# A 32-tile attention pipeline: the last tile's powers, W, corrected v and state sums left out, and H of the tile ahead of it

## The chip, the cores and the metric

The kernel runs on the 8 cores of one Trainium2 chip. Each core takes 2 of 16 sequences (4096 rows of 1024), and no core talks to another. The metric is the device time of the slowest core, in microseconds. On each core TensorE (PE) does the matmuls and transposes, VectorE (DVE), ScalarE (ACT) and GpSimd (POOL) the elementwise work and the copies out of PSUM, and SyncE's queue (SP) and POOL issue the DMAs.

## What is computed

One pre-norm layer in two halves. The attention half works in chunks of 64 rows. A softmax inside the chunk is added to a tenth of what a running state M gives, and M is updated from row to row:

```python
Mk = einsum('bhde,bhe->bhd', M, k_t)
M = M - alpha * Mk[..., :, None] * k_t[..., None, :] + beta * v_t[..., :, None] * k_t[..., None, :]
...
attn_out = einsum('bhij,bhjd->bhid', attn, vi)
mem_out = einsum('bhid,bhde->bhie', qi, M)       # M of the chunks before
chunk_out = attn_out + 0.1 * mem_out
x = x + out @ Wo.T
```

The second half is a choice of rows by a controller, 64 small two-layer experts and a scatter back. It begins when the attention half is over.

## The kernel before

`phase_a` is the attention half and `phase_b` the expert half. A tile of phase A is one chunk of both sequences of the core (128 rows), and there are NT = 32 tiles, numbered from 0. The 64 row updates of a chunk are done at once: with the strictly triangular matrix A of alpha k k', the kernel forms the powers A[1] to A[4] and B[1] to B[4] (their transposes), adds the identity (AI), and multiplies six factors onto k. This gives W, and after the last factor Wf. With H, the sum over earlier tiles, `k_by_h` gives a correction of v, and RHS is the corrected v. `state_h` and `state_m` multiply Wf and RHS into the tile's contribution to H and to M.

All engines run one software pipeline, written out by hand: the loop over i from -1 to 34 works on tile i (projections k, v, q), tile j = i-1 (`gram_and_scores`), tile u = i-2 (powers, factors 0 to 3, `row_sums`, `queries`, `values`) and tile e = i-3 (factors 4 and 5, states, and the output projection `wo_part`). So step 32 has no projections (u=30, e=29, j=31), step 33 has u=31 and e=30, and step 34 has only e=31. Each engine goes through its own list in order, and semaphores order the engines against each other.

Names that are used below:

- `power_a`, `power_b`: 32 matmuls of 64x64 into psX on PE, copied by ACT (L411, L415). `factor`: 32 matmuls into psW on PE (L630), copied to W or Wf by DVE (L829). `state_h` L642 and `state_m` L653 write psY; DVE adds them to H_sb (L868) and M_sb (L880). POOL scales M_sb into Ms_sb (L381), which `queries` reads.
- `row_sums` (L677) waits, among others, for RHS in `s_rhs`. psY is one PSUM tile, shared by `k_by_h`, `state_h`, `state_m`, `row_sums`, `queries` and `values`. ACT takes its logarithm (L475), then the exponential (L477); POOL makes Pn from them (L391); `queries` (L700) and `values` (L684) fill psY again; `o_copy` (L435, ACT) moves it to o_fm, and `wo_part` (L569, 16 matmuls of 512 columns a tile, in two halves) multiplies by Wo. DVE adds x to each half (`x1_half`, L836), and SP stores it to x1d.
- From step 33 on, rows of phase B are prepared in phase A: `choice_stats` (L118, L119, L121, DVE) and `choice_ln` (L129, L131, ACT) for tiles 0 and 1 in step 33 and 2 and 3 in step 34, `choice_norm` (L137, DVE) in step 34. In ACT's list both `choice_ln` of step 33 stand ahead of `o_copy(31)`, and the second waits for `choice_stats(1)`, which stands behind `x1_half(30, 1)` in DVE's list.
- `cast` (L354): POOL's DMAs that write the experts' weights in bf16.
- SP ends its list with a wait until the last x1 stores have landed (L324, L325). Behind it the engines meet (L938), and PE's first work of phase B is `y_turn` (L1152).

Of the kernel before, what the change touches and what calls it, by code (L numbers as in the profile page):

```python
# [140 lines left out]
def phase_a(nc, ctx, sb, ps, sem, env):  # L141
# [73 lines left out]
    with ExitStack() as pa:  # L215
# [111 lines left out]
        def pool(g):  # L327
# [28 lines left out]
            for i in range(0, NT + 3):  # L356
# [36 lines left out]
                if 0 <= j < NT:  # L393
                    g.wait_ge(s_g, j + 1)
                    g.tensor_tensor(heads(A[0][:, :]), heads(g_sb[:, :]), by_mask(mlo), ALU.mult).then_inc(s_mask, 1)
                cast(u, 6)
                if 0 <= j < NT:
                    g.tensor_tensor(heads(B[0][:, :]), heads(g_sb[:, :]), by_mask(mup), ALU.mult).then_inc(s_mask, 1)
# [3 lines left out]
        def act(s):  # L402
# [35 lines left out]
            for i in range(-1, NT + 3):  # L438
                u, e, j = i - 2, i - 3, i - 1
                proj = 0 <= i < NT  # L440
                solve = 0 <= u < NT
# [29 lines left out]
                if solve:  # L471
                    s.wait_ge(s_pden, u + 1)
                    if u > 0:
                        s.wait_ge(s_pn, u)
                    s.activation(rden[:], psY, AF.Ln).then_inc(s_lden, 1)  # L475
                    s.wait_ge(s_lden, u + 1)
                    s.activation(rden[:], rden[:], AF.Exp, scale=-1.0).then_inc(s_rec, 1)  # L477
# [3 lines left out]
                if 0 <= j < NT:  # L481
                    s.wait_ge(s_pg, j + 1)
                    s.copy(heads(g_sb[:, :]), gram_scores[:, :, 0, :]).then_inc(s_g, 1)
                    s.activation(heads(PT[j % 2][:, :]), gram_scores[:, :, 1, :], AF.Exp, scale=0.125).then_inc(s_exp, 1)  # L484
# [9 lines left out]
        def pe(t):  # L494
# [108 lines left out]
            def power_a(u, k):  # L603
# [6 lines left out]
                if k == 4 and u + 1 < NT:  # L610
                    t.wait_ge(s_g, u + 2)
                    t.wait_ge(s_exp, u + 2)
# [34 lines left out]
            def state_m(e):  # L647
                t.wait_ge(s_h, e + 1)
# [24 lines left out]
            def row_sums(u):  # L673
                t.wait_ge(s_ptm, u + 1)
                t.wait_ge(s_rhs, u + 1)
# [38 lines left out]
            for i in range(-1, NT + 3):  # L714
                u, e = i - 2, i - 3
                proj = 0 <= i < NT
                solve = 0 <= u < NT
                ends = 0 <= e < NT

# [6 lines left out]
                if ends:  # L726
                    factor(e, 4)
# [5 lines left out]
                if ends:  # L733
                    factor(e, 5)
# [7 lines left out]
                if ends:  # L742
                    state_h(e)
# [5 lines left out]
                if ends:  # L749
# [14 lines left out]
                if solve:  # L764
                    power_b(u, 3)
                    factor(u, 0)
                    row_sums(u)
# [23 lines left out]
                if solve:  # L791
                    power_b(u, 4)
                    queries(u)
# [3 lines left out]
                if solve:  # L797
                    power_a(u, 5)
                    factor(u, 3)
                    values(u)  # L800

        def dve(v):
# [48 lines left out]
            for i in range(-1, NT + 3):  # L851
                u, e = i - 2, i - 3
                proj = 0 <= i < NT
                solve = 0 <= u < NT
                ends = 0 <= e < NT
                if ends:
# [9 lines left out]
                if ends:  # L866
# [9 lines left out]
                if ends:  # L876
# [545 lines left out]
```

## Time and profile before

| what | us |
|---|---|
| median of 3 runs | 1398.43 (1396.72 to 1401.19) |
| the profiled execution, its own time | 1394.15 |
| span of its slowest core (core 5) | 1392.3 |
| spans of the 8 cores | 1382.8 to 1392.3 |
| mean granted clock of core 5 | 0.943 |
| PE, DVE, ACT, POOL busy in the span | 83%, 70%, 58%, 48% |

A row of the timeline has its start in us from the span's start, its length, engine, line, operation, output<-inputs, shapes, the count that it merges, and in brackets the idle time of the engine ahead of it with what ended it. The granted clock is TensorE's: 0.50 is 1.2 GHz and 1.00 is 2.4 GHz. Ends of matmuls are modelled; "issue" is idle time in which the engine waited for nothing that the profile shows.

### The profile page before, as it was taken

The page shows a single profiled execution, that of the slowest core. Times are in us where ns is not written, and L with a number is a line of the kernel's source. Part 1 is how long each engine was busy: PE and PEld are TensorE (multiplying, and loading weights), DVE is VectorE, ACT ScalarE, POOL GpSimd, SP SyncE. Part 2 cuts the span into 40 slices and gives each one's busy share as a digit, 9 for nine tenths or more (in the row PEclk, how much of TensorE's full clock was granted, in tenths as well). Part 3 has the DMA queues.
Part 4 walks back from the last instruction along what each step waited for, and adds up shares of the span by engine and source line. Part 5 has one row for each costly group of instructions (what it writes and reads, how often), then busy time and mean ns, then how long its engine had stood idle before and what let it go on. Part 6 is the DMA issues. An engine that isn't in the chain of part 4 may idle for free. (4 is left out here: it accounts for less than half of the span.)

```text
span 1392.3 us, 68142 instructions; the slowest of 8 cores (1382.8 to 1392.3 us)
## 1 busy us (share of the span) xinstructions
PE 1148.8 (83%) x28864; PEld 692.5 (50%) x28864; DVE 980.6 (70%) x1389; ACT 810.8 (58%) x1187; POOL 672.1 (48%) x566
## 2 busy tenths in 40 slices
PE   1578988889899988889899888885677779887798
PEld 0245555555555555555555555553344556544665
DVE  3167777677777777777777777765778587785776
ACT  0155656555565555555565555654249776488775
POOL 4166766776767766777667766675101000011000
PEclk9799999999999999999999999996569799988999
DMA  9912222222222222222222222123134485750947
GB/s 160 149 44 45 43 51 51 52 48 49 47 51 55 45 49 53 47 53 43 52 50 53 50 47 40 30 34 79 23 94 143 134 263 164 217 184 35 312 135 235
DMA packets 75158, 122.09 MB, mean 88 GB/s; under 512 B 13408, under 2 KB 38000, under 8 KB 74864
## 3 DMA queue, kind: packets, MB, share of 16 engines
q1 hardware_dynamic: 48128, 92.30, 21.8%
q0 software_dynamic: 26736, 25.44, 13.6%
q8 instruction: 237, 3.88, 1.1%
q14 instruction: 57, 0.47, 0.1%
HBM read 117.93 MB, written 41.94 MB: 115 GB/s over the span
## 5 line engine op out<-in xcount | busy, mean ns | idle before, releaser
L829 DVE CAST W<-psW 128x1024 bf16<-128x1024 f32 x160 | 195.5, 1222 | 112.6 <-PE psW L630 112.4
L415 ACT CAST B<-psXY 128x1024 bf16<-128x1024 f32 x128 | 129.9, 1015 | 74.0 <-PE psXY L597 74.0
L1095 POOL TENSOR_TENSOR psel<-permT_sb,gmask_sb 128x256 bf16<-128x256 bf16 x32 | 20.1, 628 | 260.8 <-DVE permT_sb L1327 235.9
L411 ACT CAST A<-psXY 128x1024 bf16<-128x1024 f32 x128 | 129.8, 1014 | 21.2 <-PE psXY L597 21.0
L517 PE MATMUL psD<-wv_sb,xnf 128*128 128x512 bf16 x512 | 128.8, 386 | 13.6 <-DMA wv_sb<-wvT 13.6
L540 PE MATMUL psD<-wq_sb,xnf 128*128 128x512 bf16 x512 | 128.6, 385 | 11.8 <-DMA wq_sb<-wqT 6.4
L508 PE MATMUL psD<-wk_sb,xnf 128*128 128x512 bf16 x512 | 123.6, 386 | 14.6 <-DMA wk_sb<-wkT 11.8
L825 DVE TENSOR_TENSOR AI<-A,eye 128x1024 bf16<-128x1024 bf16 x160 | 131.1, 834 | 1.8 <-ACT A L411 1.3
L569 PE MATMUL psD<-wo_sb,o_fm 128*128 128x512 bf16 x512 | 131.3, 391 | 0.7 <-issue 0.6
L376 POOL TENSOR_TENSOR kt<-kraw,rk 128x1024 bf16<-128x1024 f32 x32 | 60.8, 1902 | 134.4 <-ACT rk L461 134.4
L1108 ACT CAST R<-P 128x1024 bf16<-128x1024 f32 (+1 forms) x128 | 110.1, 905 | 8.3 <-PE P L1187 6.2
L391 POOL TENSOR_TENSOR Pn<-PT,rden 128x1024 bf16<-128x1024 bf16 x32 | 68.6, 2142 | 91.1 <-ACT rden L477 91.1
L1340 DVE CAST R<-P 128x512 bf16<-128x512 f32 x128 | 81.2, 685 | 28.5 <-PE P L1214 28.2
L597 PEld LDWEIGHTS psXY<-A,B 64*64 64x64 bf16 x5120 | 57.1, 110 | 76.0 <-issue 72.9
L597 PE MATMUL psXY<-A,B 64*64 64x64 bf16 (+1 forms) x5120 | 74.9, 194 | 17.1 <-ACT PT L484 7.9
L630 PE MATMUL psW<-W,AI 64*64 64x64 bf16 x5120 | 75.7, 197 | 14.6 <-DVE W L829 7.7
L435 ACT CAST o_fm<-psXY 128x1024 bf16<-128x1024 f32 x32 | 32.4, 1012 | 94.3 <-PE psXY L684 94.3
L1144 ACT COPY ring<-P 128x1024 bf16<-128x1024 bf16 x64 | 64.6, 1012 | 37.0 <-PE P L1228 37.0
L429 ACT CAST q_tm<-psD 128x512 bf16<-128x512 f32 x64 | 37.6, 587 | 82.1 <-PE psD L540 82.1
L363 POOL TENSOR_TENSOR PT<-PT,mj 128x1024 bf16<-128x1024 bf16 x32 | 68.4, 2136 | 30.7 <-DVE AI L825 30.7
L372 POOL TENSOR_TENSOR sq_sb<-kraw 128x1024 f32<-128x1024 f32 x32 | 60.6, 1893 | 45.9 <-ACT kraw L419 28.4
L1187 PE MATMUL P<-psel,xy 64*128 64x256 bf16 x512 | 58.6, 310 | 28.5 <-ACT R L1108 22.9
(138 smaller groups left out, 2578.7 us busy)
## 6 DMA issues: line engine op xcount, KB each, us to landing
ring<-f1d SPq DMA_DIRECT2D x64, 256.0 KB, 4.0
ring<-f2d SPq DMA_DIRECT2D x64, 256.0 KB, 5.0
out<-ring SPq DMA_DIRECT2D x64, 256.0 KB, 3.4
xy<-x SPq DMA_DIRECT2D x68, 128.0 KB, 2.4
f1d<-f1w POOLq DMA_DIRECT2D x128, 64.0 KB, 2.6
f2d<-f2w POOLq DMA_DIRECT2D x128, 64.0 KB, 2.7
x1d<-x1b SPq DMA_DIRECT2D x64, 128.0 KB, 2.4
xy<-x1d SPq DMA_DIRECT2D x32, 256.0 KB, 3.5
```

The source lines that it names most:

```text
L411: s.copy(A[k][:], psX).then_inc(s_a, 1)
L415: s.copy(B[k][:], psX).then_inc(s_b, 1)
L508: ins = t.matmul((psD0, psD1)[hf][:, :], xn_fm[i % 2][:, kc * 128:(kc + 1) * 128], wk_sb[:, kc * 1024 + hf * 512:kc * 1024 + hf * 512 + 51 ...
L517: ins = t.matmul((psD0, psD1)[hf][:, :], xn_fm[i % 2][:, kc * 128:(kc + 1) * 128], wv_sb[:, kc * 1024 + hf * 512:kc * 1024 + hf * 512 + 51 ...
L540: ins = t.matmul((psD0, psD1)[hf][:, :], xn_fm[i % 2][:, kc * 128:(kc + 1) * 128], wq_sb[:, kc * 1024 + hf * 512:kc * 1024 + hf * 512 + 51 ...
L569: ins = t.matmul((psD0, psD1)[hf][:, :], o_fm[:, oc * 128:(oc + 1) * 128], wo_sb[:, oc * 1024 + hf * 512:oc * 1024 + hf * 512 + 512], star ...
L597: ins = t.matmul(psX[c:c + 64, hr * 64:hr * 64 + width], left[k][r:r + 64, hr * 64:hr * 64 + 64], right[k][r:r + 64, hr * 64:hr * 64 + width],
L630: ins = t.matmul(psW[c:c + 64, hr * 64:hr * 64 + 64], AI[k][r:r + 64, hr * 64:hr * 64 + 64], w_old, start=True, stop=True, tile_position=( ...
L825: v.tensor_tensor(heads(AI[k][:, :]), heads(A[k][:, :]), by_mask(eye2), ALU.add).then_inc(s_ai, 1)
L829: v.tensor_copy((Wf if k == 5 else W[k % 2])[:], psW[:, 0:1024]).then_inc(s_w, 1)
L1108: s.copy(gather_place(n, q)[:, 0:h, :, :], gathered_ps(q)[:, 0:h, :, :]).then_inc(s_ga, 1)
L1340: v.tensor_copy(place(2 * p)[:, 4 * hf:4 * hf + 4, :, :], half_tiles(P[u % 3][:, 0:512])).then_inc(s_iv, 1)
```

## The change

The flag `solve` no longer holds for tile 31 and `state` (factors 4 and 5, `state_m`) no longer holds for tile 31 either; `state_h` and the sum into H stop after tile 29. `row_sums`, `queries` and `values` go by a flag of their own, `attend`, that still holds for tile 31. Two waits take the place of ones that would never be met: `row_sums(31)` waits for the sum into M_sb of tile 30 (`s_m`), and `state_m(30)` waits itself for Wf, RHS and the o_copy of tile 30. The masks A[0], B[0] of tile 31 and the copy g_sb that feeds them go as well.

```diff
@@ pool: masks of tile 31
-                if 0 <= j < NT:
+                if 0 <= j < NT - 1:
                     g.wait_ge(s_g, j + 1)
                     g.tensor_tensor(heads(A[0][:, :]), heads(g_sb[:, :]), by_mask(mlo), ALU.mult).then_inc(s_mask, 1)
...
-                if 0 <= j < NT:
+                if 0 <= j < NT - 1:
                     g.tensor_tensor(heads(B[0][:, :]), heads(g_sb[:, :]), by_mask(mup), ALU.mult).then_inc(s_mask, 1)
@@ act
-                solve = 0 <= u < NT
+                solve = 0 <= u < NT - 1
+                attend = 0 <= u < NT
...
-                if solve:
+                if attend:
                     s.wait_ge(s_pden, u + 1)
...
-                    s.copy(heads(g_sb[:, :]), gram_scores[:, :, 0, :]).then_inc(s_g, 1)
+                    if j < NT - 1:
+                        s.copy(heads(g_sb[:, :]), gram_scores[:, :, 0, :]).then_inc(s_g, 1)
@@ pe: power_a, state_m, row_sums
-                if k == 4 and u + 1 < NT:
-                    t.wait_ge(s_g, u + 2)
+                if k == 4:
+                    if u + 2 < NT:
+                        t.wait_ge(s_g, u + 2)
                     t.wait_ge(s_exp, u + 2)
...
-                t.wait_ge(s_h, e + 1)
+                if e < NT - 2:
+                    t.wait_ge(s_h, e + 1)
+                else:
+                    t.wait_ge(s_w, 6 * e + 6)
+                    t.wait_ge(s_rhs, e + 1)
+                    t.wait_ge(s_o, e + 1)
...
-                t.wait_ge(s_rhs, u + 1)
+                if u < NT - 1:
+                    t.wait_ge(s_rhs, u + 1)
+                else:
+                    t.wait_ge(s_m, u)
@@ pe: the loop
-                solve = 0 <= u < NT
+                solve = 0 <= u < NT - 1
+                attend = 0 <= u < NT
                 ends = 0 <= e < NT
+                state = 0 <= e < NT - 1
...
-                if ends:
+                if state:
                     factor(e, 4)
...
-                if ends:
+                if state:
                     factor(e, 5)
...
-                if ends:
+                if 0 <= e < NT - 2:
                     state_h(e)
...
-                if ends:
+                if state:
                     state_m(e)
...
                     factor(u, 0)
+                if attend:
                     row_sums(u)
...
+                if attend:
                     queries(u)
...
                     factor(u, 3)
+                if attend:
                     values(u)
@@ dve: the loop
-                solve = 0 <= u < NT
+                solve = 0 <= u < NT - 1
                 ends = 0 <= e < NT
-                if ends:
+                state = 0 <= e < NT - 1
+                if state:
                     v.wait_ge(s_pa, 5 * e + 5)
...
-                if ends:
+                if 0 <= e < NT - 2:
                     v.wait_ge(s_ph, e + 1)
                     v.tensor_add(H_sb[:], H_sb[:], psY).then_inc(s_h, 1)
...
-                if ends:
+                if state:
                     v.wait_ge(s_pm, e + 1)
```

How the engines' lists stand now is seen best at their ends. Line numbers of the changed kernel are higher (L569 is L571, L630 L633, L653 L661, L677 L688, L684 L695, L700 L711, L829 L846, L836 L853, L880 L898, L1152 L1170). PE's list before, from `queries(31)` to the first work of phase B:

```order
L700 MATMUL psXY<-kaq,Ms_sb 64x64 x32
L569 MATMUL psD<-wo_sb,o_fm 128x512 x8
L597 MATMUL psXY<-A,B 64x32 x32
L630 MATMUL psW<-W,AI 64x64 x32
L684 MATMUL psXY<-Pn,vt 64x64 x32
L630 MATMUL psW<-W,AI 64x64 x64
L642 MATMUL psXY<-RHS,Wf 64x64 x32
L653 MATMUL psXY<-Wf,RHS 64x64 x32
L569 MATMUL psD<-wo_sb,o_fm 128x512 x16
L938 UNCONDITIONAL_BRANCH
```

And PE's list now, from the beginning of step 33 (factors 4 and 5 of tile 30):

```order
L633 MATMUL psW<-W,AI 64x64 x64
L661 MATMUL psXY<-Wf,RHS 64x64 x32
L688 MATMUL psXY<-PT,onesblk 128x512 x2
L571 MATMUL psD<-wo_sb,o_fm 128x512 x8
L711 MATMUL psXY<-kaq,Ms_sb 64x64 x32
L571 MATMUL psD<-wo_sb,o_fm 128x512 x8
L695 MATMUL psXY<-Pn,vt 64x64 x32
L571 MATMUL psD<-wo_sb,o_fm 128x512 x16
L956 UNCONDITIONAL_BRANCH
```

The 16 matmuls of `wo_part(31)` stood behind two factors and both state products, and stand now right behind `values(31)`; ten of the fourteen groups of matmuls that stood ahead of `wo_part(30)` in step 33 are gone. DVE's list before, from `x1_half(30, 1)` on:

```order
L836 TENSOR_TENSOR x1b<-x,psD 128x512
L825 TENSOR_TENSOR AI<-A,eye 128x1024
L118 BN_STATS bst_y<-xy 128x6
L119 BN_STATS bst_y<-xy 128x6
L121 BN_AGGR mv_y<-bst_y 128x2
L858 TENSOR_TENSOR AI<-psXY,eye 128x16x32
L829 CAST W<-psW 128x1024 x2
L829 CAST Wf<-psW 128x1024
L868 TENSOR_TENSOR H_sb<-H_sb,psXY 128x1024
L880 TENSOR_TENSOR M_sb<-M_sb,psXY 128x1024
L137 TENSOR_SCALAR xy<-xy,mv_y,rstd_y 128x1024 x2
```

DVE's list now, from the last sum into M_sb (tile 30) on:

```order
L898 TENSOR_TENSOR M_sb<-M_sb,psXY 128x1024
L853 TENSOR_TENSOR x1b<-x,psD 128x512
L118 BN_STATS bst_y<-xy 128x6
L119 BN_STATS bst_y<-xy 128x6
L121 BN_AGGR mv_y<-bst_y 128x2
L853 TENSOR_TENSOR x1b<-x,psD 128x512
L118 BN_STATS bst_y<-xy 128x6
L119 BN_STATS bst_y<-xy 128x6
L121 BN_AGGR mv_y<-bst_y 128x2
L137 TENSOR_SCALAR xy<-xy,mv_y,rstd_y 128x1024 x2
```

The six operations between the choice's second statistics and its first norms are gone, and so is the AI sum between `x1_half(30, 1)` and the statistics; the order of what is left is as it was.

## Rows read from the trace of the kernel before

**Rows 1.** Timeline of core 5, end of step 33 to phase B.

```profile
991.34 1.90 PE L569 MATMUL psD<-wo_sb,o_fm 128*128 128x512 bf16 x8
...
993.35 0.69 DVE L836 TENSOR_TENSOR x1b<-x,psD 128x512 bf16<-128x512 f32 x1 [0.64 <-PE psD L569]
...
994.55 0.69 DVE L118 BATCH_NORM_STATS2 bst_y<-xy 128x6 f32<-128x512 bf16 x1
...
996.74 0.99 ACT L435 CAST o_fm<-psXY 128x1024 bf16<-128x1024 f32 x1
...
1004.84 0.64 PE L653 MATMUL psXY<-Wf,RHS 64*64 64x64 bf16 x32 [1.49 <-DVE H_sb L868]
...
1005.41 6.14 PE L569 MATMUL psD<-wo_sb,o_fm 128*128 128x512 bf16 x16
...
1011.66 0.69 DVE L836 TENSOR_TENSOR x1b<-x,psD 128x512 bf16<-128x512 f32 x1 [0.20 <-PE psD L569]
...
1014.90 1.01 PE L1152 MATMUL P<-ident_bf,xy 128*128 128x128 bf16 x8 [3.35 <-PEq L938]
```

**Rows 2.** Timeline of core 5, first part of step 33.

```profile
974.47 0.64 PE L630 MATMUL psW<-W,AI 64*64 64x64 bf16 x32 [0.86 <-DVE W L829]
...
975.23 1.23 DVE L829 CAST Wf<-psW 128x1024 bf16<-128x1024 f32 x1 [1.01 <-PE psW L630]
...
978.94 0.64 PE L653 MATMUL psXY<-Wf,RHS 64*64 64x64 bf16 x32 [0.49 <-DVE H_sb L868]
...
979.77 1.22 DVE L880 TENSOR_TENSOR M_sb<-M_sb,psXY 128x1024 bf16<-128x1024 bf16 x1 [0.37 <-PE psXY L653]
...
981.14 1.90 POOL L381 TENSOR_TENSOR Ms_sb<-M_sb,b 128x1024 bf16<-128x1024 bf16 x1 [6.92 <-DVE M_sb L880]
...
983.26 0.59 PE L677 MATMUL psXY<-PT,onesblk 128*128 128x512 bf16 x1
...
984.82 0.59 PE L677 MATMUL psXY<-PT,onesblk 128*128 128x512 bf16 x1 [0.97 <-issue]
```

**Rows 3.** Timeline of core 5, step 32: the softmax chain and a quarter of Wo.

```profile
956.81 1.03 PE L677 MATMUL psXY<-PT,onesblk 128*128 128x512 bf16 x2
...
958.00 1.02 ACT L475 ACTIVATE rden<-psXY 128x1024 f32<-128x1024 f32 x1 [0.49 <-PE psXY L677]
...
959.11 1.06 ACT L477 ACTIVATE rden<-rden 128x1024 f32<-128x1024 f32 x1
...
960.38 2.13 POOL L391 TENSOR_TENSOR Pn<-PT,rden 128x1024 bf16<-128x1024 bf16 x1 [3.04 <-ACT rden L477]
...
960.61 1.87 PE L569 MATMUL psD<-wo_sb,o_fm 128*128 128x512 bf16 x4
...
961.24 1.03 ACT L484 ACTIVATE PT<-psXY 128x1024 bf16<-128x1024 f32 x1
...
962.42 0.56 PE L597 MATMUL psXY<-A,B 64*64 64x64 bf16 x32
```

**Rows 4.** Busy time by engine, granted clock (PEclk), DMA share, GB/s in stretches of 3 us.

```profile
987.00:990.00 3.00, 3.00 (x70) 1.37 (x68) 1.41 (x2) 1.74 (x2) 2.06 (x1) 0.50 0.00 0
...
996.00:999.00 3.00, 0.65 (x32) 0.54 (x32) 1.98 (x4) 1.40 (x3) 0.00 (x0) 0.65 0.00 0
```

**Rows 5.** POOL's last casts in the timeline of core 5.

```profile
990.02 1.52 POOL L354 DMA_DIRECT2D f2d<-f2w  x3
```

**Rows 6.** DMA issues on the page: count, KB each, median us from issue to landing.

```profile
f2d<-f2w POOLq DMA_DIRECT2D x128, 64.0 KB, 2.7
```

**Rows 7.** Chain that ended last, first selection stretch of phase B: start, us, what.

```profile
1030.18 1.02 ACT R L1108
...
1035.52 1.02 ACT R L1108
...
1050.26 1.01 ACT R L1108
...
1054.34 1.00 ACT R L1108
```

## The prediction

> **What bounds the kernel now.** I read the end of phase A first, since the change touches nothing ahead of step 32. The timeline of the end of step 33 and of step 34 gives the last link: the last `x1_half` starts at 1011.66, its store has to land, the engines meet, and PE starts phase B at 1014.90, which is 3.24 us behind that start [rows 1]. Nothing of phase B can begin earlier, so phase B moves one for one with the last `x1_half`. That in turn waits for PE's `wo_part(31)`, which runs from 1005.41 to 1011.55; and this stands in PE's list behind `state_m(31)` at 1004.84 [rows 1]. Its own input o_fm was ready at 997.73, when `o_copy(31)` ended (996.74 + 0.99) [rows 1]. So 7.7 us of the tail (1005.41 - 997.73) is time in which `wo_part(31)` waits for factors and states that no later tile reads. I then followed step 33 backwards in the same way.
>
> **The change, part by part.** All times are of core 5.
>
> *Step 32.* POOL loses two masks, ACT the copy g_sb (about 1 us, as its neighbour L484). Exp(31) then starts 0.9 us earlier. `power_a(30, 4)`, which waits for it, started at 962.42; Exp ended at 962.27 and the four matmuls of Wo ahead of it on PE ended at 962.48 [rows 3]. The two covers end together, so with the first gone PE is still held by the second: I take 0. If the Wo matmuls ran at the full clock they would take about 1.0 (half of the 1.90 for eight in [rows 1]) instead of 1.87, and up to 0.8 us would be won; that is the upper bound. POOL's next operation behind the masks waits for AI[4] of tile 30, which DVE makes at the end of the step; 0.
>
> *Step 33, up to the sum into M.* The chain of factors of tile 30 alternates between PE and DVE: factor 5 starts on PE at 974.47 when DVE's copy of W is done, and Wf is copied from 975.23 to 976.46 [rows 2]. The powers of tile 31 lay in the gaps of it, so this part does not move. After it, `state_m(30)` started at 978.94, having waited for the sum into H [rows 2]. Now it waits only for Wf. An engine takes up work some 0.15 us behind another's end (POOL at 981.14 behind the sum at 980.99) [rows 2]; I allow 0.25, so it starts at 976.7. That is 2.2 us won. The sum into M follows 0.83 later (978.94 to 979.77), so from 977.55 to 978.75.
>
> *From M to Wo of tile 30.* Before, `row_sums(31)` came at 983.26 behind `k_by_h`, a power, a factor and RHS [rows 2]. Now it needs the sum into M alone: 978.9, 4.3 us earlier. In step 32 the logarithm started 1.19 us behind `row_sums`, the exponential 1.11 behind that and Pn 1.27 behind that [rows 3], which puts Pn from 982.5 to 984.6. Ms is made from 978.9 to 980.8 (1.90 in [rows 2]). PE runs the first 8 matmuls of `wo_part(30)` from 979.75. At the half clock 4 of them took 1.87 [rows 3], which with the modelled end of the last taken off is 0.43 each, so 8 take 3.4; at the full clock 8 took 1.90 with that end, so 1.75 [rows 1]. Then `queries(31)` for 0.65, then the second 8. At the half clock `wo_part(30)` ends at 987.25; at the full clock at 983.7 (the queries wait until 981.3 for the logarithm).
>
> *A wait that takes over.* `values(31)` could end by 985.3 to 988, and `o_copy(31)` behind it. But ACT has the second `choice_ln` ahead of `o_copy(31)`. Before, `x1_half(30, 1)` started at 993.35, `choice_stats(1)` at 994.55 (0.60 of that is the AI sum that now goes) and `o_copy` 2.19 later [rows 1]. From now on that is 0.60 + 2.19 = 2.8 us from `x1_half(30, 1)` to `o_copy(31)`, and another 1.2 (0.99 and a wait) until `wo_part(31)` starts, in which PE has nothing. In the kernel before this was hidden under the factors of tile 31.
>
> - Half clock throughout: `x1_half(30, 1)` 987.4, `o_copy` 990.2, `wo_part(31)` 991.35, which is 14.1 us earlier than 1005.41. 16 matmuls at 0.427 are 6.8, the last `x1_half` at 998.4, phase B at 1001.6: 13.3 us won.
> - Full clock throughout: 983.8, 986.6, 987.8; 16 matmuls take 3.5, but DVE becomes the limit: `x1_half(31, 0)` at 989.7, `choice_stats(3)` (0.6 + 1.6 us), last `x1_half` at 991.9, phase B at 995.1: 19.8 won.
>
> Which of them holds is read from the granted clock. In 987 to 990 it was 0.50 (1.2 GHz) with PE busy all three microseconds, and the next eight Wo matmuls at 991.34 ran at the full clock [rows 1, 4]; in 996 to 999, where PE was busy for 0.65 us of 3, it fell to the half clock (mean 0.65) [rows 4]. The 16 matmuls of `wo_part(31)` took 6.14, 0.9 less than 7.0 at the half clock with the modelled end, so the clock rose near their end [rows 1]. Now PE is busy without a gap from 978.9, so I expect the clock to rise at about 983 to 986, somewhere in `wo_part(30)`, to fall in or just behind the gap of 3 to 4 us ahead of `wo_part(31)`, and to rise again in it. With the rise at 983.3: `wo_part(30)` ends at 985.75, `o_copy(31)` 988.65, `wo_part(31)` from 989.85 for 5.2 to 6.2, last `x1_half` between 995.3 and 996.0, phase B at 998.5 to 999.2, 15.7 to 16.4 won. With the rise just too late for the second half of `wo_part(30)`: 13.3 to 14.5. I take the middle of the two, 15.2 us.
>
> The Trainium skill, "TensorE: Matmul & The Clock Gate", section "The HAM clock gate", says that the throttled clock is the default and that activity releases it. By that rule a kernel with less PE work keeps the half clock longer, and the sum would be the 13.3 us of the first line; the trace agrees with it in that the clock fell behind an idle stretch [rows 4].
>
> **Sum.** 2.2 (to `state_m`) + 2.1 more (to `row_sums`, together 4.3) + 10.9 more from there to phase B (in which two factors, their copies, H and M of tile 31 were 7.7, powers and factors between the Wo matmuls the rest) = 15.2. Phase B is unchanged. The profiled execution (1394.15, span 1392.3) would come to 1379.0; it lies 4.3 below the median, so against the median I predict 1398.4 - 15.2 = 1383.2.
>
> **The rivals.**
>
> - *Full clock through the tail*: 19.8 us, 1378.6. For it: Wo ran at the full clock at 991.34 [rows 1]. Against: PE has less to do ahead of `row_sums` now, and an idle gap ahead of `wo_part(31)`. 0.12.
> - *Half clock, and stalls of the sequencer on top*: PE had idle times put down to "issue" in step 33, in the middle of groups of like matmuls (0.97 between the two of `row_sums`) [rows 2]. At 13.3 less one or two such stalls of 1 to 2 us each: 9 to 12 won, 1386 to 1389. Against: PE's list now has 194 matmuls from the start of step 33 to phase B, where it had 802. 0.15.
> - *Phase A's end is held by another*: POOL's list ends with a wait for its casts. They were issued by 991.54 and land 2.7 us behind issue [rows 5, 6], so by 994.2, and they stand behind Pn in POOL's list, which should now end at 984.6: with the same 1.5 and 2.7, 988.8. That is ahead of the stores in each case. Only if the casts didn't move and landed much later would the gain stop; as no change, 1398. 0.03.
> - *The other side, a slower kernel*: in phase B's selection stretch a turn takes 5.34 us at the half clock (1030.18 to 1035.52) and 4.08 at the full clock (1050.26 to 1054.34) [rows 7]. If, entered 15 us earlier and otherwise, the stretch stayed at the half clock, each turn would cost 1.26 us more. The gain is used up after 12 turns, and the kernel is slower by over 0.3% (4.2 us) from 16 turns on; the stretch has 16 tiles in each half of phase B, about 13 of them at the full clock now, so both halves would have to lose it: 26 turns, 33 us, 1416. Phase B's own work sets its clock, so 0.02.
> - *Partly*: a wait that I don't see gives half of it back: 1391. 0.05.
>
> **How the numbers follow.** My forecast has 0.63 (13.3 to 17, that is 1381.4 to 1385.1). The others are 0.12, 0.15, 0.03, 0.02 and 0.05. A run of this kernel lies within 2 to 3 us of its median (1396.72 to 1401.19), and the slowest of eight cores counts, each with its own clock. The range that leaves out no more than 2 in 10 reaches from the full-clock case (1378.6) to one with a stall (1388): 1378.0 to 1388.3. 0.3% (4.2 us) is about what a measurement of this kernel can tell from no change. Faster by more: 0.63 + 0.12 + 0.15 + 0.05 = 0.95; I say 0.94. Within: 0.04. Slower: 0.02.
>
> **What would show the steps right or wrong.** On core 5 relative to the copy of Wf of tile 30 (then 975.23): `state_m(30)` 1.5 us behind it; `row_sums` 3.7; Pn 7.3; `o_copy(31)` between 11.4 and 15.0, ended in its wait by mv_y of DVE and not by PE; `wo_part(31)` 1.2 behind that, with a mixed clock; last `x1_half` to phase B 3.2. From Wf to phase B 24.5 us instead of 39.7. Wrong would be: `o_copy(31)` released by `values`; "issue" gaps inside the groups of step 33; a selection stretch of phase B with more turns at 0.50; or a time from the last `x1_half` to phase B above 3.5 us.

## The result and the profile after

The changed kernel took 1384.2 us (median, the fastest 1382.15), the kernel before 1397.58 in the four runs beside it. Runs in which the cores of a die ran at a lower clock (one of four of the changed kernel here, 1431.15 us) are left out of every median and ratio of this document. The ratio is 0.9897, with a 95% interval of 0.9868 to 0.9925; in a later measurement (e11) it was 0.9886 [0.9869, 0.9903]. By the means of the runs that is 14.4 us less (1383.57 for 1397.98) and 16.0 us less (1382.78 for 1398.80); the forecast was 15.2 less, 1383.2 us, in a range of 1378.0 to 1388.3.

The profiled execution took 1382.15 us itself. The page's first lines, of its slowest core (core 0): the span, and for each engine its busy time, share and instructions (PE had 28864 matmuls before, 608 more).

```profile
span 1380.5 us, 66842 instructions; the slowest of 8 cores (1365.7 to 1380.5 us)
PE 1145.0 (83%) x28256; PEld 687.5 (50%) x28256; DVE 966.6 (70%) x1373; ACT 801.9 (58%) x1178; POOL 668.3 (48%) x564
```

The timeline of core 5 (span 1373.5 us here), the core that [rows 1, 2] show, from step 33 to phase B: the columns are start, duration, engine, line, operation, and in brackets the idle time before with what ended it. Here L571 is `wo_part`, L661 `state_m`, L688 `row_sums`, L711 `queries`, L695 `values`, L435 `o_copy`, L853 `x1_half`, L1170 the start of phase B.

```profile
970.65 1.23 DVE L846 CAST Wf<-psW 128x1024 bf16<-128x1024 f32 x1 [1.01 <-PE psW L633]
972.24 0.64 PE L661 MATMUL psXY<-Wf,RHS 64*64 64x64 bf16 x32 [1.71 <-DVE Wf L846]
973.07 1.22 DVE L898 TENSOR_TENSOR M_sb<-M_sb,psXY 128x1024 bf16<-128x1024 bf16 x1 [1.19 <-PE psXY L661]
974.43 1.01 PE L688 MATMUL psXY<-PT,onesblk 128*128 128x512 bf16 x2 [1.55 <-DVE M_sb L898]
975.24 3.14 PE L571 MATMUL psD<-wo_sb,o_fm 128*128 128x512 bf16 x8
977.97 2.13 POOL L391 TENSOR_TENSOR Pn<-PT,rden 128x1024 bf16<-128x1024 bf16 x1 [0.66 <-ACT rden L478]
978.94 1.90 PE L571 MATMUL psD<-wo_sb,o_fm 128*128 128x512 bf16 x8
980.06 1.52 POOL L354 DMA_DIRECT2D f2d<-f2w  x3
980.77 0.44 PE L695 MATMUL psXY<-Pn,vt 64*64 64x64 bf16 x32
980.95 0.69 DVE L853 TENSOR_TENSOR x1b<-x,psD 128x512 bf16<-128x512 f32 x1 [0.26 <-PE psD L571]
983.23 0.29 ACT L129 ACTIVATE rstd_y<-mv_y,cst 128x1 f32<-128x1 f32 x1 [1.87 <-DVE mv_y L121]
983.73 1.00 ACT L435 CAST o_fm<-psXY 128x1024 bf16<-128x1024 f32 x1
985.09 5.04 PE L571 MATMUL psD<-wo_sb,o_fm 128*128 128x512 bf16 x16 [3.87 <-ACT o_fm L435]
990.62 0.66 DVE L853 TENSOR_TENSOR x1b<-x,psD 128x512 bf16<-128x512 f32 x1
995.38 1.01 PE L1170 MATMUL P<-ident_bf,xy 128*128 128x128 bf16 x8 [5.25 <-PEq L956]
```

`state_m` now waits for the copy of Wf, and `row_sums` for the sum into M. The row to read twice is that of ACT at 983.23. `values` ended at 981.21, but ACT took `o_copy` up at 983.73 only, behind the second `choice_ln`, which had waited 1.87 us for mv_y of DVE. So PE stood for 3.87 us ahead of `wo_part(31)`. And from the last `x1_half` (990.62) to phase B it took 4.76 us, not the 3.24 of [rows 1].

The windows of the same core: PE (with its instructions), PE's weight loads, DVE, ACT and POOL, then the granted clock, the share of time in which the DMA engines were busy, and GB/s moved.

```profile
972.00:975.00 3.00, 1.21 (x34) 0.81 (x35) 1.22 (x1) 0.00 (x0) 0.57 (x1) 0.50 0.00 0
975.00:978.00 3.00, 3.00 (x9) 0.98 (x7) 0.00 (x0) 2.08 (x2) 2.34 (x4) 0.54 0.14 17
978.00:981.00 3.00, 3.00 (x70) 1.51 (x72) 2.15 (x5) 0.22 (x1) 3.00 (x3) 1.00 0.31 70
984.00:987.00 3.00, 1.91 (x5) 0.72 (x6) 1.88 (x4) 1.22 (x3) 0.00 (x0) 0.60 0.01 2
987.00:990.00 3.00, 3.00 (x12) 1.08 (x10) 1.49 (x3) 0.00 (x0) 0.00 (x0) 0.83 0.00 0
```

The clock rose near the end of the first half of `wo_part(30)`, fell by the start of `wo_part(31)` (mean 0.60 in 984 to 987; PE had just stood for 3.87 us), and rose in it.

In what follows all times are counted from the start of DVE's copy of Wf of tile 30 and are medians over the eight cores of one execution: so what the cores differ by in the 970 us ahead of it (up to 12 us within one execution) drops out. How finely the table can be read is seen where a kernel stands in it twice: changed and e11 differ by 0.1 us at phase B, 0.4 at the last `x1_half` and 0.7 at `o_copy`, e8 and e12 by 0.2, 0.5 and less than 0.1.

| kernel | `row_sums` | Pn | `o_copy` | `wo_part(31)` | last `x1_half` | phase B | last two apart |
|---|---|---|---|---|---|---|---|
| before | 8.08 | 12.57 | 21.31 | 29.97 | 35.96 | 39.18 | 3.21 |
| changed | 3.78 | 7.32 | 13.75 | 15.10 | 20.65 | 24.22 | 3.57 |
| e1, o_copy first | 3.78 | 7.32 | 11.45 | 12.85 | 18.18 | 23.89 | 5.78 |
| e2, masks kept | 3.79 | 7.32 | 13.74 | 15.16 | 20.64 | 24.35 | 3.71 |
| e3, step 34 only | 8.05 | 12.57 | 20.97 | 22.37 | 28.00 | 31.36 | 3.23 |
| e4, H of tile 30 kept | 5.91 | 9.45 | 15.45 | 16.81 | 22.47 | 26.20 | 3.73 |
| e5, casts early | 3.79 | 7.32 | 13.39 | 14.78 | 20.25 | 23.20 | 2.93 |
| e6, e1 and e5 | 3.79 | 7.32 | 10.90 | 12.28 | 17.63 | 20.69 | 3.10 |
| e7, PE filled | 3.60 | 6.72 | 9.66 | 11.03 | 15.59 | 19.83 | 4.24 |
| e8, softmax ahead | -2.38 | 1.09 | 7.28 | 8.81 | 13.73 | 16.94 | 3.23 |
| e9, POOL longer | 3.78 | 7.32 | 11.43 | 12.84 | 18.15 | 22.52 | 4.37 |
| e10, Ms on DVE | -2.35 | 1.18 | 7.71 | 9.18 | 14.64 | 17.57 | 2.93 |
| e11, changed again | 3.78 | 7.32 | 13.05 | 14.60 | 20.28 | 24.12 | 4.07 |
| e12, as e8, timed | -2.41 | 1.18 | 7.27 | 8.83 | 14.23 | 17.14 | 2.93 |

(The last column is the median of the cores' own differences.) From before to changed the stretch is 15.0 us shorter (39.18 - 24.22). What lies behind it stayed: from phase B's first matmul to the end of the core it is 377.5 us before, 377.8 in the changed kernel and 376.8 in e11 (medians of the cores, which differ among themselves by 5 to 8 us).

### The profile page after: what moved, and what is told of

The parts are those of the page before. It is cut to its first block and busy times, and to the rows that moved or that the text cites. A ratio compares the mean times of both kernels' runs of the same rounds, so it can differ in the third digit from the quotient of the medians.

```text
span 1380.5 us, 66842 instructions; the slowest of 8 cores (1365.7 to 1380.5 us)
## 1 busy us (share of the span) xinstructions
PE 1145.0 (83%) x28256; PEld 687.5 (50%) x28256; DVE 966.6 (70%) x1373; ACT 801.9 (58%) x1178; POOL 668.3 (48%) x564
## 5 line engine op out<-in xcount | busy, mean ns | idle before, releaser
L846 DVE CAST W<-psW 128x1024 bf16<-128x1024 f32 x155 | 189.3, 1221 | 111.2 <-PE psW L633 110.9
L415 ACT CAST B<-psXY 128x1024 bf16<-128x1024 f32 x124 | 125.8, 1015 | 69.9 <-PE psXY L599 69.9
L519 PE MATMUL psD<-wv_sb,xnf 128*128 128x512 bf16 x512 | 129.0, 386 | 13.6 <-DMA wv_sb<-wvT 13.6
L411 ACT CAST A<-psXY 128x1024 bf16<-128x1024 f32 x124 | 125.8, 1014 | 20.6 <-PE psXY L599 20.1
L571 PE MATMUL psD<-wo_sb,o_fm 128*128 128x512 bf16 x512 | 130.7, 390 | 5.8 <-ACT o_fm L435 3.9
L435 ACT CAST o_fm<-psXY 128x1024 bf16<-128x1024 f32 x32 | 32.4, 1012 | 93.6 <-PE psXY L695 93.6
L633 PE MATMUL psW<-W,AI 64*64 64x64 bf16 x4960 | 73.5, 196 | 12.2 <-issue 6.1
```

Of the source, the lines that this page charges most:

```text
L411: s.copy(A[k][:], psX).then_inc(s_a, 1)
L415: s.copy(B[k][:], psX).then_inc(s_b, 1)
L519: ins = t.matmul((psD0, psD1)[hf][:, :], xn_fm[i % 2][:, kc * 128:(kc + 1) * 128], wv_sb[:, kc * 1024 + hf * 512:kc * 1024 + hf * 512 + 51 ...
L571: ins = t.matmul((psD0, psD1)[hf][:, :], o_fm[:, oc * 128:(oc + 1) * 128], wo_sb[:, oc * 1024 + hf * 512:oc * 1024 + hf * 512 + 512], star ...
L633: ins = t.matmul(psW[c:c + 64, hr * 64:hr * 64 + 64], AI[k][r:r + 64, hr * 64:hr * 64 + 64], w_old, start=True, stop=True, tile_position=( ...
L846: v.tensor_copy((Wf if k == 5 else W[k % 2])[:], psW[:, 0:1024]).then_inc(s_w, 1)
```

## The experiments

### Which part gave what: e1 to e4

Lines marked - are the changed kernel's, + the experiment's, unless said otherwise.

**e1** moves the second `choice_ln` of step 33 on ACT behind `o_copy(31)`.

```diff
                 if 0 <= e < NT:
                     o_copy(e)
+                    if i == NT + 2:
+                        choice_ln(s, env, 1)
...
                     choice_ln(s, env, 2 * (i - NT - 1))
-                    choice_ln(s, env, 2 * (i - NT - 1) + 1)
+                    if i > NT + 1:
+                        choice_ln(s, env, 2 * (i - NT - 1) + 1)
```

> The changed kernel with ACT's o_copy(31) moved ahead of the second choice_ln of step 33. My theory: in the changed kernel o_copy(31) is held by the statistics of choice tile 1 and not by values(31), so o_copy(31) comes about 2.5 us earlier against the copy of Wf of tile 30 (median of the cores 13.75 us behind its start now, then 11.3), wo_part(31) likewise, and phase B 2 to 3 us earlier (24.2 to about 21.8 behind that start). Rival, that values(31) or PE's own list holds it: nothing moves. Rival, that DVE takes over as the limit (its norms and third statistics ahead of x1_half(31, 0)): wo_part(31) is earlier, phase B by less than 1 us.

`o_copy`, `wo_part(31)` and the last `x1_half` came 2.2 to 2.5 us earlier (1.6 to 2.1 against e11), as they should; phase B came 0.3 earlier (23.89 for 24.22). The timeline and the waits of core 5, PE's and then SP's (what waited, for what, us in all, times, longest):

```profile
982.00 1.52 POOL L354 DMA_DIRECT2D f2d<-f2w  x3
984.32 1.01 ACT L435 CAST o_fm<-psXY 128x1024 bf16<-128x1024 f32 x1 [0.52 <-PE psXY L698]
985.78 3.61 PE L574 MATMUL psD<-wo_sb,o_fm 128*128 128x512 bf16 x16 [1.58 <-ACT o_fm L435]
991.04 0.66 DVE L856 TENSOR_TENSOR x1b<-x,psD 128x512 bf16<-128x512 f32 x1
```
```profile
PE P L1173 <- PEq L959: 7.0, 1, 7.0
SPq L959 <- PEq L959: 2.6, 1, 2.6
```

`o_copy` is now released by `values` (PE psXY), so the wait behind `choice_ln` was real. But SP, whose wait for the last store ended 2.6 us before the engines met, was not last any more. Both rows name PE's own queue, which had been done with its list for 7 us: a releaser by inference, and not the cause. Something else held the end of phase A, in all eight cores at the same place (23.8 to 24.4 us behind the start of the copy of Wf, with 5.34 to 7.12 from the last `x1_half` to phase B).

**e2** makes the two masks and g_sb of tile 31 again, which nothing reads.

```diff
-                if 0 <= j < NT - 1:
+                if 0 <= j < NT:
...
-                    if j < NT - 1:
+                    if j < NT:
                         s.copy(heads(g_sb[:, :]), gram_scores[:, :, 0, :]).then_inc(s_g, 1)
...
-                    if u + 2 < NT:
+                    if u + 1 < NT:
                         t.wait_ge(s_g, u + 2)
```

> The changed kernel with what it took from step 32 put back: the copy g_sb on ACT and the two masks of tile 31 on POOL. My theory: both were covered, so the time from row_sums of tile 30 to the first copy of W in step 33 stays the same within 0.3 us, and the time from the copy of Wf of tile 30 to phase B stays at 24.2 us. Rival, that Exp(31) held PE in step 32: 0.5 to 0.9 us more in step 32.

Behind Wf the two kernels are alike (24.35 and 24.22). Ahead of it, step 32 from the start of `row_sums(30)` to Wf took 18.12 us before, 18.24 in e2, 17.36 in the changed kernel and 17.30 in e11: leaving these operations out gave 0.8 us. The other runs agree: e3, which keeps them, shows 18.10, and the nine others without them 17.10 to 17.51. So the expectation of no more than 0.3 us was wrong. It did not come through Exp(31): `power_a(30, 4)` starts 5.61 us behind `row_sums(30)` before and in e2, and 5.54 and 5.52 in the other two. It lies in `queries(30)`, whose 32 matmuls took 1.55 us before, 1.73 in e2, 0.79 and 0.69 in the changed kernel and e11 (medians of the cores). The timelines of the kernel before (core 5, L700), of e2 (core 1) and of the changed one (core 5):

```profile
964.77 0.56 PE L700 MATMUL psXY<-kaq,Ms_sb 64*64 64x64 bf16 x24
966.45 0.31 PE L700 MATMUL psXY<-kaq,Ms_sb 64*64 64x64 bf16 x8 [1.12 <-issue]
```
```profile
960.67 0.56 PE L711 MATMUL psXY<-kaq,Ms_sb 64*64 64x64 bf16 x24
962.09 0.31 PE L711 MATMUL psXY<-kaq,Ms_sb 64*64 64x64 bf16 x8 [0.86 <-issue]
```
```profile
961.18 0.69 PE L711 MATMUL psXY<-kaq,Ms_sb 64*64 64x64 bf16 x32
```

The gap in the middle is an "issue" one: the profile shows nothing that PE waited for. Without the masks it is gone in most cores, not in all (core 1 of the changed kernel still has 0.54 us of it, and 1.42 for the group). POOL's casts then also go out together and earlier; whether that is why was not tried.

**e3** is the kernel before with only what belongs to tile 31 left out in step 34 (factors 4 and 5, their copies, H and M); its powers, masks and first factors are computed, and so is H of tile 30. Against the kernel before:

```diff
+                state = 0 <= e < NT - 1
...
-                if 0 <= e < NT:
+                if state:
                     factor(e, 4)
...
-                if 0 <= e < NT:
+                if state:
                     state_m(e)
```

> The kernel before with only the parts of step 34 left out (factors 4 and 5, both state products and both sums of tile 31); step 33 stays whole. My theory: wo_part(31) then starts when o_copy(31) is done, 21.3 + 1.3 = 22.6 us behind the start of the copy of Wf of tile 30 instead of 30.0, so about 7.4 us are won, and from there 5.2 to 6.2 us to the last x1_half: phase B at about 31.5 to 32 instead of 39.2. The rest of the 15 us, about 7.5, is then step 33's. Rival, that the tail's gain was given back by the clock (more of wo_part(31) at the half clock): phase B at 33 or more.

`row_sums` and Pn stay where they were (8.05, 12.57), `o_copy` within 0.4 (20.97). `wo_part(31)` comes 7.6 earlier, right behind `o_copy`, and phase B 7.8: just the 7.7 that the prediction read from [rows 1]. The other 7.2 of the 15.0 come from step 33.

**e4** computes H of tile 30 again, which only M of tile 31 would need.

```diff
             def state_m(e):
-                if e < NT - 2:
-                    t.wait_ge(s_h, e + 1)
-                else:
-                    t.wait_ge(s_w, 6 * e + 6)
-                    t.wait_ge(s_rhs, e + 1)
-                    t.wait_ge(s_o, e + 1)
+                t.wait_ge(s_h, e + 1)
...
-                if 0 <= e < NT - 2:
+                if state:
                     state_h(e)
...
-                if 0 <= e < NT - 2:
+                if state:
                     v.wait_ge(s_ph, e + 1)
```

> The changed kernel with H of tile 30 still computed (state_h(30) on PE, the sum into H on DVE, and state_m(30) behind it). My theory: both lie on the path to row_sums(31), so the sum into M starts 2.1 us later (4.54 instead of 2.42 us behind the start of the copy of Wf), and phase B comes 2.1 us later: 26.3 instead of 24.2. Rival, that later waits (Pn, choice statistics) swallow it: phase B later by less than 1 us.

M starts at 4.54 again (2.42 without H), Pn 2.13 later, phase B at 26.20: H of one tile was worth 2.0 us, nearly undiminished to the end. So of the 15.0 us 7.8 are step 34's (e3) and 2.0 are H's (e4). The other 5.2 (31.36 - 26.20) come from what else left step 33, the powers, factors 0 to 3, `k_by_h` and RHS of tile 31; no run takes these apart.

### What holds the end of phase A: e5 to e7, and e9

Two things were left for e1's lost 2.2 us: POOL, whose program ends with a wait for its last casts, and something on PE's side, which the profile names.

**e5** issues POOL's casts of step 33 (parts 3 to 7) right behind part 2, ahead of Ms and Pn; **e6** is e5 with e1's edit.

```diff
                 cast(u, 2)
+                if i == NT + 1:
+                    for part in range(3, 8):
+                        cast(u, part)
...
-                cast(u, 3)
-                cast(u, 4)
+                if i != NT + 1:
+                    cast(u, 3)
+                    cast(u, 4)
```

> The changed kernel with POOL's last five weight casts (tile 31, parts 3 to 7) issued in step 33 ahead of Ms and Pn instead of around and behind them. In the changed kernel and in e1 the last packets of POOL's casts moved 11.1 to 11.5 us ahead of phase B in every core looked at, while the time from the last x1_half to phase B went from 2.9 to 7.1 us. Theory A: POOL, with its wait for the casts, is the last to reach the meeting point; then the time from the last x1_half to phase B becomes the same short value (about 2.9 to 3.2 us) in all cores, and phase B comes at 23.6 to 23.9 behind the start of the copy of Wf instead of 24.2. Theory B: PE's sequencer is late (it is PE that the profile names), from reading its code; then the values stay spread from 2.9 to 5.2 as in the changed kernel.

> The kernel of e1 (o_copy(31) ahead of the second choice_ln) with the five casts early. Theory A (casts): the 2.5 us that e1 won at the last x1_half now reach phase B, which comes 18.2 + 2.9 to 3.2 = 21.1 to 21.4 us behind the start of the copy of Wf (23.9 in e1, 24.2 in the changed kernel). Theory A2: POOL is the last, but by its last instruction and not by the casts' landing: phase B came 13.2 us behind the end of POOL's last instruction in the changed kernel, Pn now ends at 9.45, so phase B at 22.7. Theory B (PE's code): 23.9 as in e1, with 5.3 to 7.1 us from the last x1_half.

In e5 the step from the last `x1_half` to phase B is 2.90 to 3.00 us in all cores, where it was 2.92 to 5.21, and phase B comes at 23.20. 0.4 of this 1.0 us is already in `x1_half` (20.25 for 20.65; but e11, the changed kernel again, has 20.28, so this part need not be the edit's), 0.6 is the end itself. Phase B came earlier than even theory A had it, here and in e6 (20.69 for 21.1 to 21.4). In e6 e1's gain comes through: 20.69. But in four of its cores phase B stands at 20.44 or 20.45. Core 1 of e6:

```profile
976.82 2.14 POOL L395 TENSOR_TENSOR Pn<-PT,rden 128x1024 bf16<-128x1024 bf16 x1 [1.64 <-ACT rden L487]
980.01 1.01 ACT L442 CAST o_fm<-psXY 128x1024 bf16<-128x1024 f32 x1
986.74 0.66 DVE L863 TENSOR_TENSOR x1b<-x,psD 128x512 bf16<-128x512 f32 x1
989.94 1.01 PE L1180 MATMUL P<-ident_bf,xy 128*128 128x128 bf16 x8 [4.95 <-PEq L966]
```

Pn, now POOL's last operation, ends at 978.96, and phase B comes 10.98 us behind that. In the three other cores that stand at 20.44 or 20.45 it is 10.98 too. In the remaining four it is 11.46 to 11.62, and there phase B comes 2.89 to 2.99 us behind the last `x1_half`: whichever is later. Theory A2, with 13.2 us behind POOL's last instruction, had the right engine and the wrong number; theory B is out.

**e7** is e6 with 25 matmuls into a PSUM tile that nobody reads, in PE's gaps of step 33, in five places, of which one is shown.

```diff
+            def filler(n):
+                for k in range(n):
+                    t.matmul(psX[:, 0:512], xn_fm[0][:, 0:128], wo_sb[:, 0:512], start=True, stop=True)
...
+                if i == NT + 1:
+                    filler(5)
                 if state:
                     factor(e, 5)
```

> The kernel of e6 with 25 matmuls of 512 columns added on PE in its idle times of step 33 (6 ahead of factor 4 of tile 30, 5 ahead of factor 5, 5 ahead of state_m, 4 behind it, 5 behind values(31)); their results, in psX, are read by nobody. My theory of the clock: the changed kernel ran the first half of wo_part(30) and part of wo_part(31) at 1.2 GHz since PE idled between the factors; with PE kept busy the granted clock stays near 1.0 through the tail, wo_part(30) takes 1.2 to 3.4 us less, and the last x1_half comes 1.5 to 3 us earlier than in e6. Rival: the added matmuls stand in the way of the factors (they are in PE's order) and cost as much as the clock gives back, 1 us or less either way.

Windows of e6 (core 1, copy of Wf from 969.50) and e7 (core 1, from 976.41), in each the one around the copy of Wf and the one behind it, up to `row_sums` and the start of `wo_part(30)`; the last three numbers are clock, DMA share and GB/s.

```profile
969.00:972.00 3.00, 1.02 (x63) 0.78 (x51) 1.31 (x2) 0.00 (x0) 1.60 (x4) 0.50 0.98 123
972.00:975.00 3.00, 1.72 (x5) 0.62 (x6) 1.14 (x1) 0.56 (x1) 1.72 (x1) 0.50 0.09 14
```
```profile
975.00:978.00 3.00, 2.04 (x39) 0.80 (x38) 1.81 (x2) 0.00 (x0) 2.89 (x6) 1.00 0.92 123
978.00:981.00 3.00, 2.40 (x41) 1.10 (x42) 1.22 (x1) 0.25 (x1) 0.99 (x1) 1.00 0.44 58
```

PE kept the full clock (1.00, 2.4 GHz) from the copy of Wf through `wo_part(31)`, where e6 had the half clock up to 6.4 to 8.8 us behind the start of that copy. The last `x1_half` came 2.0 us earlier than in e6 (15.59). Phase B came only 0.9 earlier and at 19.83 in all eight cores alike. From the end of Pn to phase B it is 10.97 or 10.98 us in each core: 6.72 + 2.13 + 10.98 = 19.83. The half clock, then, costs the tail about 2 us (net of what the added matmuls take), and POOL swallows over half of what a faster PE wins. The Trainium skill, "TensorE: Matmul & The Clock Gate", section "The HAM clock gate", has the throttled clock as the default that activity releases. The trace agrees: with the gaps filled the clock was 1.00 around `state_m`, without it was 0.50.

**e9** puts this to the test: e6 with one more operation behind Pn on POOL, into a tile that nobody reads.

```diff
                     g.tensor_tensor(Pn[:], PT[u % 2][:], rden[:], ALU.mult).then_inc(s_pn, 1)
+                    if i == NT + 1:
+                        g.tensor_tensor(kraw[:], PT[u % 2][:], rden[:], ALU.mult)
```

> The kernel of e6 with one more operation on POOL behind Pn of tile 31: the same product once more, written to kraw, which nobody reads (about 2.1 us). In e6 (its cores 1 and 5), e7 and e8 phase B came 10.98 us behind the end of POOL's last elementwise operation wherever the last x1_half did not end later. Theory A: 11 us pass between POOL's last work and phase B whatever the others do; phase B then comes 2.1 us later in the cores that POOL held (20.44 becomes 22.6 behind the start of the copy of Wf) and at the same 22.6 in all eight, while the last x1_half stays at 17.1 to 18.1. Theory B (PE's sequencer, or the landing of stores, is what waits): phase B stays at 20.4 to 21.1.

Core 0 of e9:

```profile
978.52 2.14 POOL L395 TENSOR_TENSOR Pn<-PT,rden 128x1024 bf16<-128x1024 bf16 x1 [1.64 <-ACT rden L489]
980.62 2.14 POOL L397 TENSOR_TENSOR kraw<-PT,rden 128x1024 f32<-128x1024 bf16 x1
988.49 0.66 DVE L865 TENSOR_TENSOR x1b<-x,psD 128x512 bf16<-128x512 f32 x1
993.73 1.01 PE L1182 MATMUL P<-ident_bf,xy 128*128 128x128 bf16 x8 [6.97 <-PEq L968]
```

Phase B came at 22.51 to 22.53 in every core, 2.1 us behind the 20.44 of the four cores of e6 that POOL held (1.8 behind the median of e6), while PE's, ACT's and DVE's operations stayed within 0.6 us of e6; from the end of kraw (982.76 here) to phase B it is 10.95 to 10.97 us in all eight. PE's program has the same instructions as in e6, so it is POOL that phase B follows. What POOL does in these 11 us the profile does not show.

### How far it goes: e8, e10, e12

**e8**, timed again as **e12**, is e6 with `row_sums(31)`, the softmax chain, Pn and the first Wo matmuls of tile 30 moved ahead of `state_m(30)`; they don't need M. Only PE's list is shown; `row_sums(31)` now waits for the o_copy of tile 30 instead of the sum into M, and POOL makes Pn ahead of Ms.

```diff
+                if i == NT + 1:
+                    factor(e, 4)
+                    row_sums(u)
+                    wo_part(e, 0, 0, 2)
+                    factor(e, 5)
+                    wo_part(e, 0, 2, 6)
+                    t.wait_ge(s_lden, u + 1)
+                    state_m(e)
+                    wo_part(e, 0, 6, 8)
+                    wo_part(e, 1, 0, 8)
+                    queries(u)
+                    values(u)
+                    continue
```

> The kernel of e6 with step 33 written in another order on PE: row_sums(31) behind factor 4 of tile 30 (the softmax chain no longer waits for the sum into M; state_m(30) waits for the logarithm instead), six of the Wo matmuls of tile 30 around factor 5, and Pn ahead of Ms on POOL. The path is then copy of Wf, state_m, M, Ms, queries, values, o_copy: o_copy(31) at 7 to 8.5 us behind the start of the copy of Wf (11.4 in e1), the last x1_half at 14 to 15.5, phase B at 17 to 18.7. If POOL's last instruction plus 13.2 us holds it, phase B not before 18.9. If PE's code holds it, not before 23.9.

> The kernel of e8 once more, timed. Phase B came 16.9 us behind the start of the copy of Wf there, 17.6 in e10, 24.2 in the changed kernel and 39.2 in the kernel before; the kernel should be 7.3 us faster than the changed one and 22 to 23 us faster than the one before (0.9 us of it from step 32): ratio 0.983 to 0.984, level with e10 or 0.6 us ahead of it. If the time doesn't follow phase B's start, it stays at the changed kernel's 0.9886.

Core 0 of e8:

```profile
972.05 0.59 PE L701 MATMUL psXY<-PT,onesblk 128*128 128x512 bf16 x2
974.34 1.23 DVE L873 CAST Wf<-psW 128x1024 bf16<-128x1024 f32 x1 [1.01 <-PE psW L646]
978.18 1.90 POOL L387 TENSOR_TENSOR Ms_sb<-M_sb,b 128x1024 bf16<-128x1024 bf16 x1 [0.30 <-DVE M_sb L925]
980.22 0.69 PE L724 MATMUL psXY<-kaq,Ms_sb 64*64 64x64 bf16 x32 [1.17 <-POOL Ms_sb L387]
981.62 1.01 ACT L445 CAST o_fm<-psXY 128x1024 bf16<-128x1024 f32 x1 [0.80 <-PE psXY L708]
983.16 5.30 PE L584 MATMUL psD<-wo_sb,o_fm 128*128 128x512 bf16 x16 [1.66 <-ACT o_fm L445]
```

`row_sums` now stands ahead of Wf and the chain through Ms is the long one. POOL's last operation is now Ms. In four cores phase B comes 10.98 us behind its end (at 16.46 to 16.72), in the other four 2.92 to 2.96 behind the last `x1_half` (at 17.15 to 17.18): the two bounds meet, with a median of 16.94 (17.14 in e12, where POOL holds one core alone). That is just ahead of the 17 to 18.7 expected, and rules out both 13.2 us behind POOL and PE's code. Timed, the ratio is 0.9834 [0.9807, 0.9861] (1376.34 us against 1400.40), the best of this study with e10.

**e10** is e8 with Ms of tile 30 given to DVE, right behind its sum into M.

```diff
                     v.tensor_add(M_sb[:], M_sb[:], psY).then_inc(s_m, 1)
+                    if e == NT - 2:
+                        v.wait_ge(s_m, e + 1)
+                        v.tensor_tensor(Ms_sb[:, :].rearrange("p (s a c) -> p s a c", s=2, a=8),
...
```

> The kernel of e8 with Ms of tile 30 made by DVE right behind the sum into M instead of by POOL, so that POOL's last work is Pn, which ends near 3.2 us behind the start of the copy of Wf. POOL then allows phase B from 14.2 on and is out of it; DVE makes Ms in 1.2 us instead of POOL's 1.9, but x1_half(30, 0) stands behind it. Theory: phase B at 15.8 to 16.6 (16.9 in e8, 24.2 in the changed kernel), 7.6 to 8.4 us faster than the changed kernel, near 1376 us where the kernel before takes 1398: ratio 0.983 to 0.985. Rival: DVE is the limit of the tail by now, and the 1.2 us are lost there: phase B at 17 or more.

Phase B came at 17.57, no earlier than e8's 16.94, so the hoped for 15.8 to 16.6 was missed, and phase B came where the rival had it. POOL was free (its last operation ended 13.6 to 14.4 us ahead of phase B), but the last `x1_half` came at 14.64 (13.73 in e8, 14.23 in e12). Core 2 of e10, with the copy of Wf from 968.80:

```profile
974.80 0.45 PE L708 MATMUL psXY<-Pn,vt 64*64 64x64 bf16 x32
976.01 0.29 ACT L129 ACTIVATE rstd_y<-mv_y,cst 128x1 f32<-128x1 f32 x1 [6.44 <-DVE mv_y L121]
976.51 0.99 ACT L445 CAST o_fm<-psXY 128x1024 bf16<-128x1024 f32 x1
```

`values(31)` came 0.7 us earlier than in e8 (6.00 for 6.72 behind the start of the copy), so the faster Ms did reach it. But `o_copy(31)` came 0.4 later (7.71 for 7.28): it stands in ACT's list behind the first `choice_ln` too, and that one now waited for the statistics of choice tile 0, which DVE reached 1.3 us later. In all eight cores of e8 and of e12 `o_copy` waited 0.8 to 0.9 us for `values`, in all eight of e10 it did not wait for it. It is the wait of the changed kernel once more, one `choice_ln` further ahead; moving this one behind `o_copy` as well was not tried. Timed it was 0.9836 [0.9821, 0.9852], 1375.61 us, no different from e12.

**e11** is the changed kernel, timed again beside e9 and e10.

> The changed kernel as it is, once more in more rounds on the chip of the last kernels, for a narrower ratio. By phase B's move (24.2 instead of 39.2 us behind the start of the copy of Wf, 15.0 us) it should be 14 to 16 us faster than the kernel before, ratio 0.989 to 0.990. Phase B at 23.7 to 24.8 behind the copy in all cores.

Its ratio is 0.9886 [0.9869, 0.9903] (medians 1383.3 against 1399.1 us), phase B at 24.12. It stands for the changed kernel against e10, whose interval lies wholly below: the edits of e10 together (casts, `choice_ln`, PE's order, Ms) won another 0.5%.

## Why the prediction was right

- *`state_m(30)` 2.2 us earlier, `row_sums` 4.3*: 2.12 and 4.30 (8.08 - 3.78), and e4 shows that H is what gave the first. Pn was expected at 7.3 and came at 7.32.
- *The wait that takes over*: `o_copy(31)` was held by `choice_ln` and mv_y, as said, at 13.75 (11.4 to 15.0 was given), and `wo_part(31)` 1.35 behind it (1.2). e1 removes the wait and `o_copy` comes 2.3 earlier (1.6 against e11).
- *The clock*: it rose in `wo_part(30)`, fell by the start of `wo_part(31)` and rose in it, which is the case between the two lines. e7 shows the size: 2.0 us at the last `x1_half` for a full clock. The rival of a full clock through the tail (19.8) did not come, nor that with added stalls of the sequencer: behind the copy of Wf of tile 30 none of the eight cores has an idle row put down to "issue", where the kernel before has three or more in each.
- *The tail of step 34, 7.7 us*: 7.6 in e3.
- *Wf to phase B in 24.5 (39.7 before)*: 24.22, 24.12 in e11, for 39.18; on core 5 itself 24.73 for 39.67. *Phase B unchanged*: within 1 us, as said above.
- *Step 32 at 0, at most 0.8*: mis-sized; it gave 0.8. The reasoning about Exp held (`power_a(30, 4)` moved by less than 0.1), but the time was in a gap of PE's issue inside `queries(30)`, which the prediction did not look at.
- *"Phase A's end is held by another"*: the step that failed. The prediction let phase B move one for one with the last `x1_half`, at 3.2 us, and named a time above 3.5 as a sign of being wrong. It was 3.57 in the median and 4.76 in core 5 (4.07 in e11's median). The rival had 0.03, from POOL being done when its casts have landed, at 988.8. In these runs phase B came no sooner than 11.0 us behind POOL's last elementwise operation, or, where its casts go out last as in the changed kernel, some 11.4 us behind their last packet (11.35 to 11.45 in all cores of the changed kernel, e1, e4 and e11). In the kernel before this was covered: there the last packet had moved 19.4 to 21.9 us ahead of phase B. The change used that cover up. In the changed kernel it cost 0.6 to 1.0 us (e5), and it was too small to show in the time beside the 0.8 that came from step 32. Whoever had gone on from here by the profile's own releasers would have lost e1's 2.2 us without knowing why.

The sum: 15.0 in the stretch and 0.8 in step 32 are 15.8, where the two measurements give 14.4 and 16.0. That the forecast of 15.2 fell so close is in part luck. Two omissions had opposite signs: 0.8 us won in step 32, and 0.6 to 1.0 us lost to POOL at the meeting of the engines. And 15.2 was no case of its own but the middle between a late and an early rise of the clock (nearer 15.0 by its own bounds of 13.3 and 16.4). Without POOL's hold, in e5, the stretch is 16.0 us shorter (39.18 - 23.20), within the 15.7 to 16.4 of the early rise; what POOL kept brought the sum back to near the middle. The chain and the order of the clock's rises and falls came as worked out.

## What to carry to other kernels

Work of the last round that no later round reads is worth what stands behind it in order, not its busy time: follow the chain from the last instruction back and look at each engine's list for what is queued ahead (here a `choice_ln` ahead of `o_copy` kept 1.6 to 2.3 us of it). Where all engines meet, ask of each one when it comes free, also of those off the path, and check it by making that engine later on purpose; the releaser that a profile infers at such a place may be an engine long done. Short stretches in a long kernel are best compared from a common event, as a median over the cores: phase B's start repeated within 0.2 us there, where whole times scatter by 3 us.

## What the runs showed of the hardware

- Phase B never came sooner than 10.95 to 10.98 us behind the end of POOL's last elementwise operation, and stood just there in 25 cores of five runs (4 of e6, 8 of e7, 8 of e9, 4 of e8, 1 of e12), whether that operation was Pn, Ms or the added one. Where POOL was earlier, it came 2.9 to 3.0 us behind the last `x1_half` (3.2 in the kernel before and in seven cores of e3; what the 0.3 there is stays open). Core 5 of e3 has 3.50: the last packet of its casts moved 11.66 us ahead of phase B, the distance of all eight cores of e2 (11.64 to 11.69), so POOL held it. Where the 11 us go is open too.
- A group of 32 like matmuls can hold a gap (0.86 and 1.12 us in the rows shown) in which PE waited for nothing that the profile shows. It was there more often with the masks of POOL and the copy of ACT than without (group medians 1.55, 1.73 and 1.77 us in the kernel before, e2 and e3; 0.69 to 0.85 in the others). What causes it is open.
- 25 matmuls whose results nobody reads held the full clock in all eight cores and made the last `x1_half` 2.0 us earlier, net of the time that they took themselves.
